# Softmax stage of a two-layer graph network: gathers of neighbour rows issued two at a time, each behind a wait for the landing of the one two places ahead

## The reference, cut to what matters

```python
h = lrelu(node_features @ w_W + w_b)
edge_h = lrelu(edge_features @ ew_W + ew_b)
h_i, h_j = h[tgt], h[nbr]
e_ij = jnp.concatenate([h_i, h_j, edge_h], axis=-1) @ a_W + a_b
seg_max = jax.ops.segment_max(e_ij, tgt, num_segments=N)
ex = jnp.exp(e_ij - seg_max[tgt])
alpha = ex / jax.ops.segment_sum(ex, tgt, num_segments=N)[tgt]
out = jax.ops.segment_sum(alpha * h_j, tgt, num_segments=N)
return lrelu(out)                      # then added to x and layer-normed
```

## Time and profile before

| what | value |
|---|---|
| median of 3 runs | 6498.25 us (6482.75 to 6502.19) |
| the profiled execution: span on the core | 6510.1 us, 11.9 us over the median |
| softmax stage, first gather to the end | 3831.6 to 6510.1 us |
| of it, first to last start of a gather | 3831.6 to 6462.1 us, 1700 gathers |
| PE, DVE, ACT, POOL busy, share of the span | 64%, 54%, 29%, 54% |

### The profile page before, as it was taken

How to read it: one execution, slowest core, us unless ns; L and a number is a source line. 1 busy time by engine, 2 the same in 40 slices (tenths; PEclk the granted TensorE clock), 3 DMA queues, 4 the chain that set the end, 5 groups by cost and what they waited for, 6 DMA issues and landing times. The chain is left out here.

```text
span 6510.1 us, 83702 instructions
## 1 busy us (share of the span) xinstructions
PE 4187.0 (64%) x17113; PEld 3084.5 (47%) x17114; DVE 3490.4 (54%) x11262; ACT 1870.4 (29%) x5506; POOL 3530.3 (54%) x3618
## 2 busy tenths in 40 slices
PE   3767777776777777777777835555555555555555
PEld 2545555554555545555555524444444444444444
DVE  6555556555555555565556644444444444444444
ACT  2222222222222222222222213333333333333333
POOL 3555555554555545555555426666666666666664
PEclk8888888988898888888888867777777777777777
DMA  3444444443444434444444623333333333533332
GB/s 115 116 115 119 113 117 125 116 115 111 120 116 119 118 110 116 113 122 114 114 116 125 110 62 91 92 91 91 92 90 92 93 92 90 91 90 93 91 91 69
DMA packets 546631, 679.29 MB, mean 104 GB/s; under 512 B 341873, under 2 KB 379359, under 8 KB 546221
## 3 DMA queue, kind: packets, MB, share of 16 engines
q0 software_dynamic: 172416, 464.26, 26.7%
q1 hardware_dynamic: 359216, 201.09, 11.8%
q10 hardware_dynamic: 14976, 13.69, 0.6%
HBM read 648.41 MB, written 29.43 MB: 104 GB/s over the span
## 5 line engine op out<-in xcount | busy, mean ns | idle before, releaser
L750 POOL DMA_INDIRECT rows<-in_x,picked x1785 | 1789.7, 1003 | 1692.3 <-ACT picked L942 1138.5
L1658 POOL DMA_INDIRECT nbr<-nodetab,nbr_idx x1700 | 1609.8, 947 | 1030.1 <-issue 460.5
L781 PE MATMUL bank<-w_edge,feats 128*128 128x258 f32 x3264 | 1122.3, 434 | 631.0 <-ACT bank L923 360.4
L796 PE MATMUL bank<-rows,hot 128*128 128x320 f32 x3570 | 1358.4, 480 | 54.2 <-issue 47.3
L1688 PE MATMUL bank<-nbr,w 128*128 128x258 f32 x3400 | 1044.3, 471 | 289.2 <-issue 152.6
L923 ACT COPY bank<-b_edge 128x258 f32<-128x258 f32 x1635 | 610.4, 378 | 2113.9 <-DVE unused L1151 1597.1
L1151 DVE SCALAR_TENSOR_TENSOR unused<-bank,a_relu 128x258 bf16<-128x258 f32 x1632 | 686.2, 422 | 952.3 <-remote 522.8
L1688 PEld LDWEIGHTS bank<-nbr,w 128*128 128x128 f32 x3400 | 803.3, 244 | 487.6 <-issue 195.5
L781 PEld LDWEIGHTS bank<-w_edge,feats 128*128 128x128 f32 x3264 | 622.9, 213 | 861.1 <-ACT bank L923 416.5
L1720 ACT ACTIVATE w<-off,logit 128x128 f32<-128x128 bf16 x1700 | 523.6, 388 | 1490.5 <-DVE logit L1791 1146.8
L796 PEld LDWEIGHTS bank<-rows,hot 128*128 128x128 f32 x3570 | 759.4, 214 | 277.0 <-issue 126.4
(11 more groups left out here) (347 smaller groups left out, 3943.4 us busy)
## 6 DMA issues: line engine op xcount, KB each, us to landing
feats<-in_edge SPq DMA_DIRECT2D x408, 256.0 KB
rows<-in_edge SPq DMA_DIRECT2D x255, 128.0 KB, 2.6
rows<-in_x,picked POOLq DMA_INDIRECT x1785
nbr<-nodetab,nbr_idx POOLq DMA_INDIRECT x1700
rows<-in_edge SPq DMA_DIRECT2D x153, 160.0 KB
nodetab<-tab ACTq DMA_DIRECT2D x52, 129.0 KB
x_blk<-in_x SPq DMA_DIRECT2D x52, 128.0 KB
x_rows<-u_n ACTq DMA_DIRECT2D x52, 128.0 KB
```

The lines of the kernel that those rows point to most:

```text
L750: pool.indirect_dma_start(out=rows[:, STARTS[j] + s, 0:D], out_offset=None, in_=a["x"], in_offset=bass.IndirectOffsetOnAxis(ap=picked[j][: ...
L781: mm(y, feats[:, f0 * P:(f0 + 1) * P], w_edge[:], start=False, stop=True, skip_group_check=True).then_inc(o["y_ready"], 1)
L796: ins = mm(S_PS, hot[j % HR][:, s - STARTS[j], :], rows[:, s, :], start=(s == 0), stop=(s == SA - 1), skip_group_check=True)
L1658: pool.indirect_dma_start(out=nbr[:, TOFF[u] + k, :], out_offset=None, in_=nodetab, in_offset=bass.IndirectOffsetOnAxis(ap=nbr_idx[u][:, k ...
```

## The change

One semaphore per group becomes two semaphores that take turns over the tiles of a pass. Before tile t of a pass is gathered, GpSimd waits until tile t-2 has landed (for the first two tiles of a pass, the last two of the pass before). No more than two gathers are so under way. The waits for the indices and for the used rows stand once in front of each group. Who waited for the semaphore of a group (SyncE and VectorE) now waits for its last two tiles, on both semaphores.

```diff
-            nbr_in = [sem(f"nbr_in{u}", ctx) for u in range(TURN)]
+            nbr_in = [sem(f"nbr_in{r}", ctx) for r in range(2)]
...
+            def landed(i, t):
+
+                return nbr_in[t % 2], i * (CH // 2 * 16) + (t // 2 + 1) * 16
+
+            def landed_group(i, u):
+
+                return [landed(i, TOFF[u] + GROUPS[u] - n) for n in (2, 1)]
...
-                        wait_alone(sp, (nbr_in[u], i * (GROUPS[u] * 16)))
+                        wait_alone(sp, *landed_group(i - 1, u))
                         sp.dma_start(nbr_idx[u][:], nbr_all[:, bass.ds(t + TOFF[u], GROUPS[u])]).then_inc(idx_in[u], 16)
...
                     for u in range(TURN):
+                        wait_alone(pool, (idx_in[u], i * 16 + 16), (summed[u], i))
                         for k in range(GROUPS[u]):
-
-                            wait_alone(pool, (idx_in[u], i * 16 + 16), (summed[u], i))
+                            t = TOFF[u] + k
+                            wait_alone(pool, landed(i, t - 2))
                             pool.indirect_dma_start(
                                 out=nbr[:, TOFF[u] + k, :], out_offset=None, in_=nodetab,
                                 in_offset=bass.IndirectOffsetOnAxis(ap=nbr_idx[u][:, k:k + 1].bitcast(U32), axis=0),
-                            ).then_inc(nbr_in[u], 16)
+                            ).then_inc(nbr_in[t % 2], 16)
...
-                    dve.wait_ge(nbr_in[u], (i + 1) * (GROUPS[u] * 16))
+                    for on, count in landed_group(i, u):
+                        dve.wait_ge(on, count)
```

## The result

The changed kernel takes 7004.48 us (median of 4, 6971.55 to 7022.36), the kernel before 6500.22 us beside it (median of 4). The ratio is 1.0774, 95% interval 1.0742 to 1.0806: 7.7% slower. The forecast was 6950 us, 7.0%, with a range of 6720 to 7060.

A forecast was written before the change was run, and what follows sets the result against it. The loop of PE, DVE and ACT bounds the softmax stage before, POOL's queue after. 3907.47 + 2939 for 1665 gathers + 85 late + 32 tail gives 6963, less 11.9 us over the median: 6950 us, range 6720 to 7060.

The forecast's parts named there:

- The bound before: Softmax stage: the loop of PE, DVE and ACT, not POOL, sets the pace, 1.534 us per gather against POOL's beat of 1.25.
- The removed waits and the second semaphore: Repeated group waits on POOL and one more semaphore for DVE and SP: taken as 0, at most 25 us for the semaphore.
- (a): Softmax stage, from a gather's start to its landing being seen: 2.72 us, bounds 2.34 and 2.88.
- (b): Softmax stage, from POOL seeing a landing to the start of the next gather: 0.81 us.
- The rule against the row: Skill's fit puts a gather's transfer at 2.30 us, giving an end near 6520 us; the forecast kept the trace's 2.72 us.
- (c): Softmax stage: two gathers per 3.53 us, 1.765 us each; POOL's queue sets the pace and swallows 561 us of border pauses.
- (d): Late landings of a pass's last gather and beside the `x1_cur` load: 100 of 0.85 us, 85 us, bounds 0 and 100.
- The end: From the last gather to the kernel's end: 32 us in place of 48.0, as the other engines have caught up.
- rival 4: Slower by more: SP's 2.88 us in full gives 3.69 us a pair and 7084 us; chance above 7060 us 0.06.
- rival 1: Faster: 579 us of pauses before `best` go, other engines reach 7 us a group; needs pairs below 3.07 us; chance 0.04.
- Rivals 2 and 3: Landing seen after some 2.3 us, time within some 20 us of 6498, chance 0.03; or 2.34 us, below 6720, 0.09.

The follow-up runs named there:

- the last experiment: The change with the store cut to 16 of 106 rows and lanes without an edge gathering different rows: 5876.84 us, ratio 1.1884 to the kernel before.

## Why the prediction was right

**The bound before** was read rightly for the profiled place and no other. There the loop of the other engines sets 1.534 us per gather; where TensorE's results come at once, POOL's beat of 1.25 us does. The same change is 7.7% and 8.8% slower at the one kind of place and 20.3% at the other, by the same mechanism, as its own pace stays at 1.85 us.

**The removed waits and the second semaphore**, taken at 0: the group waits alone give a ratio of 0.9997, and four under way, which has all of the edit and more semaphores, 1.0004 at its place.

**(a) and (b), the round.** Predicted 2.72 + 0.81 = 3.53 us; the chain shows 2.77 + 0.77 = 3.54, and the median over the stage is 3.555. Over 1665 intervals the 0.025 us are 21 us. That the two stand in series was an assumption for which the run with one under way is the evidence (3.53 us a gather).

**The rule against the row.** The estimate of 2.30 us by the Trainium skill's fit (page "DMA: Bandwidth & Descriptors", section "Anatomy of one DMA — SWDGE (gpsimd) path") fell short: the last packet comes 2.44 us after the start (median over the stage's records), and the release that POOL acts on 2.77 us. The difference of 0.47 us in a round of two gathers would have been 0.235 x 1665 = 390 us of the sum.

**(c) POOL sets the pace, the border pauses are swallowed.** Right: no gather of the stage is released by "remote" or by TensorE any more. The mean distance of two starts, 1.853 us, lies above the 1.77 to 1.82 that the prediction wanted to see; that is the late rounds under (d). One premise was wrong: the first pass was put to last until 3907.47 as before, and it ended at 3888.19. Before, that start waited for TensorE, and TensorE was late itself: "remote" waits of 7.7 to 9.8 us had held up VectorE's copies ahead of the first group. After, the same copies were not held up (the first line is before, the others are after):

```profile
3870.26 0.69 DVE L1758 COPY r_at<-bank 128x512 f32<-128x512 f32 x1 [9.81 <-remote]
```

```profile
3829.81 3.68 DVE L1767 COPY r_at<-bank 128x512 f32<-128x512 f32 x6 [1.08 <-PE bank L1715]
...
3857.92 4.88 PE L1697 MATMUL bank<-nbr,w 128*128 128x258 f32 x14 [0.69 <-ACT w L1740]
```

So TensorE had used the first rows by 3862.8 in place of 3906.7, long before POOL came to them, and the pass lasted 69.0 us at POOL's own rounds, from a start that was 12.4 us earlier (3819.2 for 3831.6).

**(d) The late landings** were mis-sized and one was laid to the wrong transfer. Forecast 100 of 0.85 us, 85 us. What the rounds have above the median round adds up to 125 us (0.150 us by 1665 / 2). Of this 73 us are the store of 106 rows and the empty lanes, as the last experiment measured. The rest, some 50 us, are scattered rounds, which no term had; the load of `x1_cur`, which the prediction named, is worth some 4 of them at most. The last gather of a pass was rightly suspected, but why was not known: its empty lanes all read one row.

**The end.** The tail is 32.1 us, predicted 32. The execution profiled lies at its median (span 7004.9 for 7004.5) and not 11.9 us above.

The sum: 6951 - 19 (first pass) + 21 (round) + 40 (late ones) + 12 (span to median) = 7005, against 7004.48. That the first pass and the round cancel is luck; without the 19 us the time would still lie in the range. The upper end of the range is not what the prediction says of it: SP's full 2.88 us gives 7084 by its own rival 4, not 7060.

**The rivals.** The "remote" pauses before `best` did go, all 579 us, as rival 1 supposed, and nobody gained, since a round of 3.54 us is over the 3.07 at which that case decides. Rivals 2 and 3 would have needed a landing seen 0.3 us and more sooner.

**Open.** Why TensorE's results are seen up to 14 us late at some places, and why they come at once in the softmax stage with two gathers under way and not with four. The ends of matmuls in the rows are modelled, so the rows do not even tell a late release from matmuls that themselves ended later. What differs between the places is open too: two jobs on the chip with the same number had 6368 and 4946 us for the kernel before. Its stage is some 460 us longer at the one than at the other (2594 us between first and last gather in the job of 6368 us, 2136 us in the run with the group waits alone); how much of this the late results make was not shown. Three under way was run only where there was nothing to free. Its stage took 2267 us there; if TensorE's results came at once with three as well, it would by that number save some 330 us at the other places (an estimate). That was not measured. No kernel run here beats the one before.

## What to carry to other kernels

A limit on transfers under way costs next to nothing as long as its depth times the pace that the kernel would have without it covers one whole round, from a start to the landing seen and on to the next start behind the wait: here 3.55 us, against 2.5 us for two and 3.75 for three at POOL's beat. The round has to be the late one, not the usual one: the three under way still lost 2.7% to 149 late rounds. Four lost nothing, but they ran only where the other engines set a pace of 1.54 us, and some of them still waited. Price such a wait by rows that already show the two halves, an engine seen waiting for such a landing and the same instruction behind a counted wait, and look at which bound the kernel has at each place that it will run: the same edit cost 8% and 20%.

## What the runs showed of the hardware

- A counted wait on GpSimd ahead of an indirect DMA, if it is still open when GpSimd comes to it, costs 0.72 us of "issue" between the sequencer's step and the start, 0.77 us from the release. Where the landing is there in time, the wait costs nothing: with three under way 1551 of 1700 gathers start at the usual beat behind such a wait.
- A gather's round is the same with one under way as with two, 3.53 and 3.55 us. The last packet has landed 2.44 us after the start, the waiting engine is released after 2.77 us.
- A store of 106 rows of 1 KB, issued beside a gather, holds the landing of that gather back by 1.45 us and of the next by 0.45; cut to 16 rows it holds back nothing.
- A gather in which many lanes read the same row lands 0.8 us later (round 4.36 for 3.55 us); with a row of its own for each lane it does not.
- Results of TensorE were seen up to 14 us late beside a stream of gathers 1.5 us apart, at some places and not at others, and at the same places not at all in this stage with gathers 1.85 us apart and two under way. The cause is open.
